# First expert layer computed batch by batch, with its returns gathered by token and the second block's first queries made beneath it

## The chip, the cores and the metric

The kernel runs on one core of one Trainium2 chip. The time is the device time of one execution in microseconds. The kernel before took 311.76 us (median of three runs: 332.05, 311.76, 310.14). Engines are called by the profile's names: PE is the matrix engine, DVE the vector engine, ACT the activation engine, POOL the general engine that here also issues the indexed DMAs, SP the engine that issues plain DMAs.

## The reference

Input x is 2 batches of 512 tokens of 128 values; the context is 2 batches of 77 tokens. Four layers follow each other, each added to x:

```
x = x + xattn0(layernorm(x), ctx)   # 16 heads of 8, rotary, distance bias, gated output
x = x + moe0(layernorm(x))          # 8 experts, 2 of them per token, no capacity limit
x = x + xattn1(layernorm(x), ctx)   # 16 heads of 8, plain
x = x + moe1(layernorm(x))          # 8 experts, 2 per token, capacity 321 rows per expert
```

An expert is `silu(x @ w1) @ w2` with w1 128x512 and w2 512x128. The first expert layer has biases and softmax weights over the two chosen logits:

```
gates = x @ Wg + bg
weights, indices = top_k(gates, 2); weights = softmax(weights)
h = silu(einsum('bsd,edf->bsef', x, W1) + b1)
all_out = einsum('bsef,efd->bsed', h, W2) + b2
out = sum(take_along_axis(all_out, indices) * weights)
```

There is no limit on how many tokens an expert gets, so the kernel holds a slower path for more than its buffers hold. On these inputs the reference's own routing of the first expert layer sends at most 173 tokens of batch 0 and 194 of batch 1 to one expert.

## The kernel before

Tokens lie in 8 tiles of 128, taken in 4 groups of 2 tiles (`GROUPS`); groups 0 and 1 are batch 0, groups 2 and 3 batch 1. Attention runs over 16 units (`UNITS`), 4 units of 4 heads for each group. In each unit PE makes scores, DVE takes their maxima (line 814, the row `peak`), PE makes shifted scores, ACT takes the exponential (line 669) and PE multiplies by the values (line 1224). The engines' instruction streams are written out separately and meet at semaphores. Tables (`PE_STEPS`, `DVE_STEPS`, `ACT_STEPS`, `POOL_STEPS`) say how many turns after a group's last unit a step of that group is put in each engine's stream: dividing by the sum and projecting (`attended`, `project`), the residual, the normalised input of the expert layer (`hidden`), its transpose (`turn`), the gate logits, `choose` (the two experts), `ranks` (a token's place in its expert's list), `slots`, and `send`. Every engine executes its stream strictly in order, so a step that waits holds everything written behind it.

An expert layer then goes so. POOL's `send` (line 527) scatters the rows, tile by tile, into a table `sent` in device memory with 384 rows per expert, each row carrying its pair number. When all 16 sends have landed, SP loads each expert's 384 rows. PE transposes them (line 1418), DVE splits them in a high and a low part (lines 988, 990), PE makes 12 matmuls of 384 columns (line 1431) and, after ACT's silu (line 706), the second product of 3 chunks by 4 (line 1442; each float32 matmul shows as two records). DVE adds the bias and POOL scatters the results by pair number into a table `back` (line 573). When all 24 scatters have landed SP loads `back` (`xe<-back`), and DVE combines (lines 1030, 1034), normalises, and the second block's queries are made: tokens transposed, projected, split (`low`), and stacked (line 1344). Then the second attention begins. All of it is strictly one after the other for the whole of both batches, except that the second block's keys are made before the experts. `overflows` reads the fullest expert's count behind the experts and branches over the slow path if it is at most 384.

The second block's w1 and w2 are loaded once the first experts are through; ACT copies a high part of w1 (line 642) and POOL makes the low part (line 542) inside the second attention.

## Time and profile before

| what | us |
|---|---|
| profiled execution, device time | 307.54 |
| its span in the trace | 305.8 |
| median of the three runs | 311.76 |
| PE busy | 231.1 (76% of the span) |
| DVE busy | 158.0 (52%) |
| ACT busy | 115.9 (38%) |
| POOL busy | 143.2 (47%) |

Busy shares are means over stages. The page's slices show PE almost full in both attentions and both expert layers, and nearly idle between an attention and its experts and between the first experts and the second attention. The chain of waits is the view that says what such a gap waits for. Times inside the kernel are microseconds from the span's start.

### The profile page before, as it was taken

The numbers are of one execution on the slowest core, as the hardware profiler recorded it, in microseconds if no ns is written. First come the engines' busy times: TensorE is split into PE (matmuls) and PEld (weight loads), VectorE is DVE, ScalarE is ACT, GpSimd is POOL, SyncE is SP. The second block draws the span as 40 slices with busy tenths as digits, with TensorE's granted clock in tenths as the row PEclk, the third lists the DMA queues.
The fourth block names the chain that finished last, engine by engine and source line by source line (L and its number), as shares of the span: only waits on it lengthen the run. The fifth ranks groups of instructions, "written<-read, shape, count | busy, mean of one in ns | idle before, by whom it ended". The sixth has DMA issues, their size and how long they took to land.

```text
span 305.8 us, 5311 instructions
## 1 busy us (share of the span) xinstructions
PE 231.1 (76%) x1952; PEld 187.6 (61%) x1952; DVE 158.0 (52%) x503; ACT 115.9 (38%) x202; POOL 143.2 (47%) x203
## 2 busy tenths in 40 slices
PE   2776799998935468999953878899987169999900
PEld 1655676766623358999952665556555059999900
DVE  2887446486585464434212864477986222343206
ACT  4024547765401025252500167975721104424200
POOL 5634800881533731565661500681567711655640
PEclk9999999999975559999995899999999758999985
DMA  7999990200000135000015920100011161001115
GB/s 227 298 196 380 273 205 11 72 3 0 28 17 27 45 95 139 23 28 16 31 44 150 390 85 2 53 18 2 17 37 35 36 166 53 27 28 34 32 44 174
DMA packets 26962, 27.07 MB, mean 89 GB/s; under 512 B 3208, under 2 KB 23987, under 8 KB 26677
## 3 DMA queue, kind: packets, MB, share of 16 engines
q1 hardware_dynamic: 23941, 21.64, 26.0%
q0 software_dynamic: 2560, 4.08, 4.1%
q10 hardware_dynamic: 432, 0.98, 1.0%
q8 instruction: 17, 0.28, 0.4%
q14 instruction: 12, 0.10, 0.1%
HBM read 16.82 MB, written 10.79 MB: 90 GB/s over the span
## 4 chain that ended last, share of the span: by engine, by line
PE 51%; DVE 18%; DMA 9%; issue 8%; POOL 7%; ACT 5%; POOLq 1%; SPq 0%; DVEq 0%; ACTq 0%
PE ps L1442 14%; PE ps L1431 11%; PE ps L1224 6%; PE ps L1201 5%; DVE stats L793 2%; PE ps L1156 2%; DMA xres<-x 2%; PE ps L1207 2%; POOL sent L527 2%; DMA xe<-back 2%; PE ps L1176 2%; PE ps L1418 2%; DMA sent<-hidk,slotu 2%; DVE norm L1030 1%; PE ps L1247 1%
## 5 line engine op out<-in xcount | busy, mean ns | idle before, releaser
L573 POOL DMA_INDIRECT back<-probT,pairu x48 | 46.5, 969 | 34.6 <-DVE probT L1001 15.1
L1442 PE MATMUL ps<-w,hT 128*128 128x128 f32 (+1 forms) x384 | 45.0, 274 | 0.0
L1442 PEld LDWEIGHTS ps<-w,hT 128*128 128x128 f32 (+1 forms) x384 | 44.2, 183 | 0.0
L1156 PE MATMUL ps<-blank,identr 128*128 128x256 f32 x90 | 27.7, 466 | 19.1 <-DMA sent<-hidk,slotu 10.3
L669 ACT ACTIVATE probT<-ps 77x1024 f32<-77x1024 f32 x32 | 32.6, 1020 | 24.8 <-PE ps L1207 16.8
L527 POOL DMA_INDIRECT sent<-hidk,slotu x32 | 32.0, 1000 | 17.5 <-issue 9.2
L542 POOL TENSOR_TENSOR w1lo<-hT,w1hi 128x256 fp32r<-128x256 f32 x32 | 23.8, 751 | 34.7 <-ACT w1hi L642 32.7
L814 DVE TENSOR_REDUCE peak<-ps 128x8 fp32r<-128x616 f32 x32 | 25.4, 794 | 23.3 <-PE ps L1176 23.1
L1156 PEld LDWEIGHTS ps<-blank,identr 128*128 128x128 f32 x90 | 20.5, 237 | 23.6 <-issue 11.3
L1201 PE MATMUL ps<-qst,kst 100*78 100x256 f32 x128 | 29.2, 301 | 4.2 <-ACT qst L652 3.4
L706 ACT ACTIVATE hT<-ps 128x321 f32<-128x321 f32 x32 | 14.1, 441 | 33.5 <-PE ps L1431 33.3
L706 ACT ACTIVATE hT<-ps,col 128x384 f32<-128x384 f32 x32 | 17.2, 582 | 22.7 <-PE ps L1431 22.7
L1201 PEld LDWEIGHTS ps<-qst,kst 100*78 100x78 f32 x128 | 16.8, 148 | 13.5 <-ACT qst L652 12.8
L1431 PE MATMUL ps<-xhi,w1hi 128*128 128x384 f32 (+1 forms) x64 | 22.8, 357 | 1.5 <-DVE xlo L990 1.5
L1431 PE MATMUL ps<-xhi,w1lo 128*128 128x384 f32 (+1 forms) x64 | 21.5, 335 | 0.0
L1431 PE MATMUL ps<-xlo,w1hi 128*128 128x384 f32 (+1 forms) x64 | 21.5, 335 | 0.0
L1224 PE MATMUL ps<-probT,vpad 77*32 77x256 f32 x256 | 20.4, 391 | 0.5 <-ACT cst L664 0.5
L509 POOL TENSOR_SCALAR vare<-mv 128x2 f32<-128x2 f32 (+2 forms) x17 | 3.8, 226 | 35.2 <-DVE mv L796 35.2
L1224 PE MATMUL ps<-probT,onepad 77*32 77x256 f32 x256 | 19.7, 379 | 0.0
L1001 DVE TENSOR_TENSOR probT<-ps,row 128x128 f32<-128x128 f32 x24 | 7.0, 291 | 24.1 <-PE ps L1442 24.1
L1004 DVE COPY probT<-ps 128x128 f32<-128x128 f32 (+1 forms) x24 | 7.0, 290 | 22.8 <-PE ps L1442 22.8
L1207 PE MATMUL ps<-btok,bkey 98*78 98x128 f32 x128 | 17.3, 229 | 0.0
(166 smaller groups left out, 450.6 us busy)
## 6 DMA issues: line engine op xcount, KB each, us to landing
sent<-blank SPq DMA_DIRECT2D x16, 193.5 KB, 8.4
xe<-sent SPq DMA_DIRECT2D x16, 193.5 KB, 4.1
back<-blank SPq DMA_DIRECT2D x16, 128.0 KB, 5.6
hT<-w1b SPq DMA_DIRECT2D x4, 512.0 KB, 6.0
w<-w2b SPq DMA_DIRECT2D x1, 2048.0 KB, 13.1
xe<-back SPq DMA_DIRECT2D x8, 256.0 KB, 3.6
hT<-w1d SPq DMA_DIRECT2D x4, 512.0 KB, 4.3
w<-w2d SPq DMA_DIRECT2D x1, 2048.0 KB, 10.3
```

Of the source, the lines that this page charges most:

```text
L527: pool.indirect_dma_start(sent[m], bass.IndirectOffsetOnAxis(ap=slotu[:, t, k:k + 1], axis=0), hidk[:, t, k, :], None, bounds_check=NSLOT ...
L542: part = pool.tensor_tensor(w, raw[:, k % RAWS, e, half], w1hi[:, PIECE * k + e, half].bitcast(F32), ALU.subtract)
L573: pool.indirect_dma_start(back[m], bass.IndirectOffsetOnAxis(ap=pairu[0:n, e, c:c + 1], axis=0), ye[0:n, e, c, :], None, bounds_check=NPAI ...
L669: act.activation(probT[0:KV, u % RING].rearrange("p (i q) t -> p i (q t)", i=2), ps[0:KV, BK:BK + 2, :], ACT.Exp).then_inc(s_exp[a], 1)
L706: act.activation(hT[:, e % 2, f, 0:CAP[m]], ps[:, 2 + n % 4, 0:CAP[m]], ACT.Silu, bias=bias).then_inc(s_silu[m], 1)
L814: dve.tensor_reduce(peak[:, u % 2], s, AX.X, ALU.max, negate=True).then_inc(s_peak[a], 1)
L1156: pe.matmul(ps[:, bank, 0:GQ], ident, blank[:, 0:2, 0:D], start=True, stop=True)
L1201: last = pe.matmul(ps[0:KP, BK + q // 2, GQ * (q % 2):GQ * (q % 2) + GQ], kst[0:ST + Q4, b, Q4 * j + q, :], qst[0:ST + Q4, j, at:at + GQ], ...
L1207: last = pe.matmul(ps[0:KP, BK + q // 2, o:o + P], bkey[0:LOW + NEAR, t, :], btok[0:LOW + NEAR, t, :], start=False, stop=(i == GT - 1))
L1224: last = pe.matmul(ps[32 * q:32 * q + 32, BND, den * GQ:den * GQ + GQ], w, probT[0:KV, u % RING, q, :], start=(j == 0 and not den), stop=( ...
L1431: last = pe.matmul(ps[:, 2 + n % 4, 0:EVEN[m]], w[:, e, f * P:(f + 1) * P], x[:, e % 2, 0:EVEN[m]], start=(i == 0), stop=(i == len(parts) ...
L1442: last = pe.matmul(ps[0:n, 6 + k % 2, c * P:(c + 1) * P], hT[:, e % 2, f, c * P:c * P + n], w2[:, e, f, :], start=(f == 0), stop=(f == FC ...
```

## The change

- The first expert layer works batch by batch, with tables `sent_b` of 8 x 208 rows for each batch (`CAP_B`, two chunks of 104 rows). An expert of one batch is cut in two halves (`half`); 18 halves make a batch. The list `TAIL` puts batch 0's halves between the last steps of groups 2 and 3 and the second block's keys. Batch 0's rows are sent earlier (`POOL_STEPS`, send 10 and 9 turns behind, and the steps ahead of it earlier to match).
- The list `SECOND` puts the sums, norms, tokens, queries and stacks of groups 0 and 1 of the second block between batch 1's halves. Those of groups 2 and 3 come inside the second attention (turns 5 to 11), where units 8 and 9 are no longer scored ahead.
- Results are written by slot into `made_b` with plain DMAs by SP, and POOL gathers each token's two rows (`fetch`, 16 indexed DMAs) into SBUF. The pair numbers, the 24 scatters and the 4 loads of `back` of the first layer are gone. A token without a slot gets the zero row behind the table.
- The count of the fullest expert of a batch is read in the middle of `TAIL`; the branch over the slow path stands between the two batches and compares with 208.
- The copy of the rows by ACT and the warm-up matmuls around the first experts are gone. The softmax weight comes from POOL as a power of e. The weight splits move to other turns (`HIGH_TURNS`, `LOW_TURNS`).
- The second expert layer is as before.

PE at the end of the first attention (`ps` is the accumulator, `xe` the experts' rows, `hT` the hidden values). Before, all steps of all groups come first, then warm-ups, and the experts:

```order
L1301 MATMUL ps<-khi,identr 32x156 x2
L1301 MATMUL ps<-klo,identr 32x156
L1156 MATMUL ps<-blank,identr 128x256 x3
L1418 MATMUL ps<-identr,xe 128x128 x6
L1431 MATMUL ps<-xhi,w1hi 128x384
L1431 MATMUL ps<-xlo,w1hi 128x384
L1431 MATMUL ps<-xhi,w1lo 128x384
L1431 MATMUL ps<-xhi,w1hi 128x384
```

Now the last group's projection is followed at once by batch 0's rows, and ranks of group 2 come between its halves:

```order
L1371 MATMUL ps<-qhi,qlo 128x256
L1372 MATMUL ps<-sqw,attT 128x256
L1502 MATMUL ps<-identr,xe 128x104 x4
L1510 MATMUL ps<-xhi,w1hi 128x208
L1510 MATMUL ps<-xlo,w1hi 128x208
L1510 MATMUL ps<-xhi,w1lo 128x208
...
L1401 MATMUL ps<-picked,tri 128x8
L1401 MATMUL ps<-picked,ones 128x8
L1401 MATMUL ps<-picked,tri 128x8
L1502 MATMUL ps<-identr,xe 128x104 x2
```

Batch 0's experts moved ahead of the routing of groups 2 and 3. The overflow branch of PE, behind the experts before, now has batch 1's rows behind it.

DVE in the second attention. Before, the first units stand among stackings, and no combining is left:

```order
L814 TENSOR_REDUCE peak<-ps 128x8
L974 SCALAR_TENSOR_TENSOR qlo<-ps,col,qhi 128x256
L814 TENSOR_REDUCE peak<-ps 128x8
L980 CAST qst<-ps 96x2x256
L814 TENSOR_REDUCE peak<-ps 128x8
L980 CAST qst<-ps 96x2x256
L814 TENSOR_REDUCE peak<-ps 128x8 x6
L823 RECIPROCAL cst<-cst 128x256
L824 TENSOR_TENSOR attT<-cst 128x256
```

Now the combination of group 2 (`norm<-xe,wtok,xres`, `xres<-xe,wtok,norm`) stands behind the sixth unit's maxima, and its norm and `qlo` behind the next two:

```order
L916 TENSOR_REDUCE peak<-ps 128x8 x6
L1152 SCALAR_TENSOR_TENSOR norm<-xe,wtok,xres 128x128 x2
L1156 SCALAR_TENSOR_TENSOR xres<-xe,wtok,norm 128x128 x2
L895 BN_STATS stats<-xres 128x6 x2
L898 BN_AGGR mv<-stats 128x2 x2
L916 TENSOR_REDUCE peak<-ps 128x8
L908 TENSOR_SCALAR norm<-xres,mv,rstd 128x128 x2
L916 TENSOR_REDUCE peak<-ps 128x8
L1073 SCALAR_TENSOR_TENSOR qlo<-ps,col,qhi 128x256
L1079 CAST qst<-ps 96x2x256
```

Combining, normalising and splitting moved in among the maxima; group 3's copy of the same follows at turn 8.

POOL behind the sends of the first layer (`L567`, `L573`: pair numbers and scatters). Before:

```order
L527 DMA sent<-hidk,slotu 3072x129 x4
L509 TENSOR_SCALAR vare<-mv 128x2
L510 TENSOR_TENSOR rstd<-vare,power 128x2
L527 DMA sent<-hidk,slotu 3072x129 x8
L567 CAST pairu<-xe 128x3 x8
L573 DMA back<-probT,pairu 2048x128 x24
L509 TENSOR_SCALAR vare<-mv 128x2
L510 TENSOR_TENSOR rstd<-vare,power 128x2
```

Now:

```order
L582 DMA sent_batch<-hidk,slotu 1664x128 x8
L604 TENSOR_TENSOR wexp<-euler,wdif 128x8
L597 DMA xe<-made_batch,slotu 128x128 x8
L560 TENSOR_SCALAR vare<-mv 128x2
L561 TENSOR_TENSOR rstd<-vare,power 128x2
L560 TENSOR_SCALAR vare<-mv 128x2
L561 TENSOR_TENSOR rstd<-vare,power 128x2
L597 DMA xe<-made_batch,slotu 128x128 x8
L560 TENSOR_SCALAR vare<-mv 128x2
L561 TENSOR_TENSOR rstd<-vare,power 128x2
```

The gathers of batch 0 (8) and batch 1 (8) took the place of 24 scatters, and the two variances of each batch stand behind that batch's gathers.

The diff, cut to its core:

```diff
+SB = 2
+PB = 104
+CAP_B = SB * PB
+NSLOT_B = E * CAP_B
+GB = GROUPS // B
...
-PE_STEPS = [dict(project=4, turn=8, logits=9, ranks=10, next_context=8, next_parts=10, next_keys=11,
-                 turn3=6, logits3=8, ranks3=9),
-            dict(project=4, turn=7, logits=7, ranks=9)]
-DVE_STEPS = [dict(attended=5, projected3=6, residual3=6, hidden3=8, projected=7, residual=7, hidden=9,
-                  choose=11, slots=12, next_context=12, next_parts=13, next_keys=14, choose3=10, slots3=11),
-             dict(attended=5, residual=7, hidden=8, choose=10, slots=11)]
-ACT_STEPS = [dict(tanh3=4, tanh=5, copies=8, turned=8),
-             dict(copies=9, turned=7)]
-POOL_STEPS = [dict(deviation=9, residual=12, send=14),
-              dict(deviation=5, residual=7, send=10)]
+PE_STEPS = [dict(ranks=(9, 7.5, 0, 0), project=(3.5, 3.5, 4.5, 0), turn=(6, 6, 0, 0), logits=(6.5, 6.5, 0, 0)),
+            dict(project=(6, 4, 4, 4), turn=(9, 7, 7, 7), logits=(9, 7, 7, 7), ranks=(10, 9, 9, 9))]
+DVE_STEPS = [dict(choose=(9, 8, 0, 0), slots=(10, 8, 0, 0), attended=(4, 4, 4, 0), projected=(6, 6, 6, 0),
+                  residual=(6, 6, 6, 0), hidden=(7, 7, 0, 0)),
+             dict(attended=(5, 5, 5, 5), residual=(9, 7, 7, 7), hidden=(10, 8, 8, 8), choose=(11, 10, 10, 10),
+                  slots=(12, 11, 11, 11))]
+ACT_STEPS = [dict(tanh=(4, 4, 5, 0), turned=(6, 6, 0, 0)),
+             dict(copies=(11, 9, 9, 9), turned=(9, 7, 7, 7))]
+POOL_STEPS = [dict(deviation=(6, 6, 0, 0), send=(10, 9, 0, 0)),
+              dict(deviation=(7, 5, 5, 5), residual=(9, 7, 7, 7), send=(12, 10, 10, 10))]
...
+              [(8.5, "tokens", 2), (9, "queries", 2), (9.5, "stack", 2),
+               (10.5, "tokens", 3), (11, "queries", 3), (11.5, "stack", 3)]]
...
+               [(5, "sum", 2), (6, "norm", 2), (7, "low", 2), (7, "stack", 2),
+                (8, "sum", 3), (9, "norm", 3), (10, "low", 3), (10, "stack", 3)]]
...
+TAIL = [("numden", 3), ("hidden", 2), ("attended", 3), ("turn", 2), ("turned", 2), ("logits", 2), ("project", 3), ("tanh", 3),
+        ("choose", 2), ("half", 0), ("half", 1), ("ranks", 2), ("projected", 3), ("residual", 3), ("slots", 2), ("half", 2),
+        ("half", 3), ("hidden", 3), ("turn", 3), ("turned", 3), ("half", 4), ("logits", 3), ("choose", 3), ("half", 5),
+        ("ranks", 3), ("slots", 3), ("half", 6), ("half", 7), ("next_context", 0), ("half", 8), ("most", 0), ("half", 9),
+        ("next_parts", 0), ("half", 10), ("half", 11), ("next_keys", 0), ("half", 12), ("half", 13), ("half", 14),
+        ("own_keys", 0), ("half", 15), ("half", 16), ("own_keys", 1), ("half", 17)]
...
+SECOND = [("half", 0), ("half", 1), ("half", 2), ("half", 3), ("half", 4), ("sum", 0), ("half", 5), ("half", 6), ("half", 7),
+          ("norm", 0), ("tokens", 0), ("half", 8), ("sum", 1), ("queries", 0), ("high", 0), ("half", 9), ("low", 0),
+          ("half", 10), ("stack", 0), ("half", 11), ("norm", 1), ("tokens", 1), ("half", 12), ("queries", 1),
+          ("high", 1), ("half", 13), ("low", 1), ("half", 14), ("stack", 1), ("half", 15), ("half", 16), ("half", 17)]
...
+LOW_TURNS = [[4, 5, 6, 10], [9, 11, 13, 17]]
...
+        sent_b = [nc.dram_tensor(f"sent_batch{b}", (NSLOT_B, D), F32, kind="Internal").ap() for b in range(B)]
+        made_b = [nc.dram_tensor(f"made_batch{b}", (NSLOT_B + 1, D), F32, kind="Internal").ap() for b in range(B)]
...
+            def rows_to_experts(b, e):
+
+                if b >= 1:
+                    sp.wait_ge(s_xT[0], E * (b - 1) + e + 1)
+                sp.dma_start(rows_b[:, e, :, :], sent_b[b][e * CAP_B:(e + 1) * CAP_B, :]
+                             .rearrange("(c p) d -> p c d", p=PB)).then_inc(s_xe[e], 16)
+
+            def rows_made(b, e):
+
+                sp.wait_ge(s_ye[0], SB * (E * b + e + 1))
+                sp.dma_start(made_b[b][e * CAP_B:(e + 1) * CAP_B, :].rearrange("(c p) d -> p c d", p=PB),
+                             ye_b[:, b, e, :, :]).then_inc(s_made[b], 16)
+
...
+            sp.wait_ge(s_sent_b[0], 16 * TB * K2)
+            for e in range(E):
+                rows_to_experts(0, e)
+            for e in range(PIECES):
+                rows_made(0, e)
+            sp.wait_ge(s_sent_b[1], 16 * TB * K2)
+            for e in range(PIECES):
+                rows_to_experts(1, e)
+            for e in range(PIECES, E):
+                rows_made(0, e)
+                rows_to_experts(1, e)
+            for e in range(E):
+                rows_made(1, e)
+            sp.wait_ge(s_down[0], SB * E * B)
+            for k in range(RAWS):
+                first_weights(1, k)
+            sp.dma_start(w2[:], w2d.rearrange("p (e c d) -> p e c d", e=E, c=FC)).then_inc(s_w2[1], 16)
+            for k in range(RAWS, PIECES):
+                first_weights(1, k)
+            sp.wait_ge(s_sum[0], TILES)
+            sp.wait_ge(s_sent, 16 * NPAIR // P)
...
+            def fetch(g):
+
+                b = g // GB
+                pool.wait_ge(s_made[b], 16 * E)
+                if g == 0:
+                    pool.wait_ge(s_blank_b, 16 * (E + 1) * B)
+                for i in range(GT):
+                    for k in range(K2):
+                        t = GT * g + i
+                        pool.indirect_dma_start(got_b[b][:, t % TB, k, :], None, made_b[b],
+                                                bass.IndirectOffsetOnAxis(ap=slotu[:, t, k:k + 1], axis=0),
+                                                bounds_check=NSLOT_B, oob_is_err=False).then_inc(s_fetched[g], 16)
+
+            def weights():
+
+                pool.wait_ge(s_dif[0], GROUPS)
+                pool.tensor_tensor(wexp[:], euler[:], wdif[:], ALU.pow).then_inc(s_wexp[0], 1)
 
             def residual(g):
...
+            send(0, 2)
+            send(0, 3)
+            weights()
+            for b in range(B):
+                for g in range(GB * b, GB * b + GB):
+                    fetch(g)
+                for g in range(GB * b, GB * b + GB):
+                    deviations(of_group(g))
             route(1)
...
+                    if a == 1 and u == RING // B:
+                        act.wait_ge(s_made[1], 16 * E)
...
+                    dve.scalar_tensor_tensor(out=slotu[:, s, :], in0=slot[:, s, :], scalar=float(NSLOT_B), in1=over[:, s, :],
+                                             op0=ALU.min, op1=ALU.max).then_inc(s_slot[m], 1)
...
+            def half(b, h):
+
+                e, second = divmod(h, 2)
+                if h == 0:
+                    split_rows(0, E * b, ps[:, ROWS, 0:CAP_B], CAP_B)
+                if not second:
+                    if e >= 2:
+                        batch_outputs(b, e - 2)
+                    if e + 1 < E:
+                        split_rows(0, E * b + e + 1, ps[:, ROWS, 0:CAP_B], CAP_B)
+                elif e == E:
+                    batch_outputs(b, E - 1)
...
+            def raised(m, x, e, f, bank, columns):
+
+                parts = ((w1hi, xhi), (w1hi, xlo), (w1lo, xhi))
+                for i, (w, rows) in enumerate(parts):
+                    last = pe.matmul(ps[:, bank, 0:columns], w[:, e, f * P:(f + 1) * P], rows[:, x % 2, 0:columns],
+                                     start=(i == 0), stop=(i == len(parts) - 1))
+                last.then_inc(s_up[m], 1)
+
+            def lowered(m, x, e, first, n, out):
+
+                for f in range(FC):
+                    last = pe.matmul(out, hT[:, x % 2, f, first:first + n], w2[:, e, f, :], start=(f == 0), stop=(f == FC - 1))
+                last.then_inc(s_down[m], 1)
+
+            def half(b, h):
+
+                e, second = divmod(h, 2)
+                x = E * b + e
+                if h == 0:
+                    if b == 0:
+                        pe.wait_ge(s_w2[0], 16)
+                        pe.wait_ge(s_w1lo[0], PIECES)
+                        pe.wait_ge(s_exp[0], UNITS)
+                        pe.wait_ge(s_nd[0], GROUPS)
+                    rows_in(x)
+                if not second and e + 1 < E:
+                    rows_in(x + 1)
+                for f in (2 * second, 2 * second + 1) if e < E else ():
+                    n = FC * x + f
+                    pe.wait_ge(s_xTsb[0], x + 1)
+                    if n >= UPS:
+                        pe.wait_ge(s_silu[0], n - UPS + 1)
+                    raised(0, x, e, f, UP + n % UPS, CAP_B)
+                if second and e >= 1:
+                    pe.wait_ge(s_silu[0], FC * x)
+                    for c in range(SB):
+                        k = SB * (x - 1) + c
+                        if k >= 2:
+                            pe.wait_ge(s_ye[0], k - 1)
+                        lowered(0, x - 1, e - 1, c * PB, PB, ps[0:PB, DOWN + k % 2, 0:D])
+
+            def keys(a, n):
+                stack_k(0)
+
+            fullest_of = []
+            steps = dict(most=lambda a, n: fullest_of.append(fullest(pe)), project=project, turn=turn, logits=logits, ranks=ranks, next_context=next_context,
+                         next_parts=next_parts, next_keys=next_keys, half=half, tokens=tokens_in, queries=project_q,
+                         stack=stack_q, keys=keys)
 
...
+                    query_steps(a, u + 2.5)
+                    if u + 1 == second and a == 1:
+                        scores(a, second)
+                        attend(a, second - AHEAD)
+                        maxima(a, second)
+                        scores(a, second + 1)
...
+            with pe.If(fullest_of[0] > CAP_B):
```

## Rows read from the trace of the kernel before

**Rows 1.** Windows; after the span of each: engine busy us, granted clock, DMA share, GB/s.
```profile
core 0: us, PE busy (x) PEld busy (x) DVE busy (x) ACT busy (x) POOL busy (x), PEclk, DMA share, GB/s
84.00:86.00 2.00, 1.35 (x20) 0.68 (x19) 1.80 (x9) 0.58 (x1) 0.16 (x1) 1.00 0.10 33
...
88.00:92.00 4.00, 1.40 (x4) 1.23 (x5) 3.04 (x7) 0.00 (x0) 2.17 (x3) 0.50 0.05 17
...
108.00:111.50 3.50, 2.07 (x24) 1.31 (x18) 1.08 (x6) 1.36 (x3) 1.45 (x2) 0.50 0.12 38
```

**Rows 2.** Timeline of PE, end of first attention to experts: start, us, engine, line, work [idle].
```profile
84.73 0.61 PE L1224 MATMUL ps<-probT,onepad 77*32 77x256 f32 x8
...
116.53 0.44 PE L1431 MATMUL ps<-xhi,w1hi 128*128 128x384 f32 x1 [0.95 <-DVE xlo L990]
```

**Rows 3.** Chain of waits in order of time: start, us, what ran.
```profile
124.35 2.12 PE ps L1431 x12
...
129.47 2.12 PE ps L1431 x12
...
151.73 5.37 PE ps L1442 x48
...
160.17 2.18 DMA back<-probT,pairu
162.37 3.47 DMA xe<-back
...
176.99 1.19 PE ps L1344 x8
...
264.86 1.82 PE ps L1431 x12
```

**Rows 4.** Timeline of PE inside the first attention.
```profile
44.50 0.29 PE L1207 MATMUL ps<-btok,bkey 98*78 98x128 f32 x2
44.63 0.29 PE L1201 MATMUL ps<-qst,kst 100*78 100x256 f32 x1
```

**Rows 5.** Timeline of DVE, end of the first block.
```profile
76.06 0.79 DVE L814 TENSOR_REDUCE peak<-ps 128x8 fp32r<-128x616 f32 x1
...
100.89 0.17 DVE L868 SCALAR_TENSOR_TENSOR logit<-ps,gbias 128x16 f32<-128x16 f32 x1 [2.33 <-PE ps L1265]
...
104.02 0.16 DVE L898 TENSOR_TENSOR slotu<-slot,over 128x4 uint32<-128x4 f32 x1
```

**Rows 6.** Timeline of POOL, sends of the last two groups.
```profile
99.36 1.07 POOL L527 DMA_INDIRECT sent<-hidk,slotu  x1 [2.47 <-DVE slotu L898]
...
108.79 0.97 POOL L527 DMA_INDIRECT sent<-hidk,slotu  x1 [0.30 <-issue]
```

**Rows 7.** Timeline of DVE, combining the first block.
```profile
157.12 0.29 DVE L1001 TENSOR_TENSOR probT<-ps,row 128x128 f32<-128x128 f32 x1 [0.60 <-PE ps L1442]
165.86 0.61 DVE L1030 SCALAR_TENSOR_TENSOR norm<-xe,wtok,xres 128x128 f32<-128x128 f32 x2 [8.44 <-DMA xe<-back]
...
167.84 0.58 DVE L1030 SCALAR_TENSOR_TENSOR norm<-xe,wtok,xres 128x128 f32<-128x128 f32 x2
```

**Rows 8.** Timeline of DVE, second attention and tail.
```profile
180.47 0.79 DVE L814 TENSOR_REDUCE peak<-ps 128x8 fp32r<-128x616 f32 x1
...
197.86 0.80 DVE L814 TENSOR_REDUCE peak<-ps 128x8 fp32r<-128x616 f32 x1 [1.58 <-PE ps L1176]
...
217.08 0.79 DVE L814 TENSOR_REDUCE peak<-ps 128x8 fp32r<-128x616 f32 x1
...
238.95 0.56 DVE L898 TENSOR_TENSOR slotu<-slot,over 128x4 uint32<-128x4 f32 x1
```

**Rows 9.** Timeline of POOL, low weights of the second block.
```profile
193.01 12.79 POOL L542 TENSOR_TENSOR w1lo<-hT,w1hi 128x256 fp32r<-128x256 f32 x16 [17.10 <-ACT w1hi L642]
```

**Rows 10.** Page, DMA issues: line's work, count, KB each, us from issue to landing.
```profile
w<-w2d SPq DMA_DIRECT2D x1, 2048.0 KB, 10.3
...
back<-probT,pairu POOLq DMA_INDIRECT x48, 2.2
```

610 lines of the change are left out of this document (313 added, 297 removed).

## The prediction

> **What bounds the kernel now.** I read the page's slices first, then the chain of waits, then the timelines of the engines around the places that the chain names. No engine is the bound over the whole span; it changes by stage. In both attentions and both expert layers PE is nearly full. Between them it is starved. The first such gap runs from PE's last product of the first attention to the first matmul of an expert, 85.3 to 116.5 us [rows 2]. In it PE does little, and its granted clock falls from 1.00 to 0.50, which is 1.2 instead of 2.4 GHz [rows 1]. The chain shows why: the last two groups must be projected, routed and sent, and eight sends of POOL at 9.43 / 7 = 1.35 us each stand at the end [rows 6]. The second gap runs from DVE's last expert output at 157.4 to the first maxima of the second attention at 180.5 [rows 7, 8]. It holds the last scatter's landing and the reload (160.2 to 165.8, [rows 3]), then four combinations 2.0 us apart [rows 7], and the norms, queries and stacks. Together the gaps are some 54 us. The change fills both with expert work of the other batch, and pays for it in matmuls and in the second attention.
>
> **The price of an expert of one batch.** Before, an expert takes 129.47 - 124.35 = 5.12 us of PE [rows 3]. An up matmul of 384 columns costs 2.12 / 12 = 0.177 us and one of 322 columns 1.82 / 12 = 0.152 [rows 3]. The line through both gives 0.106 at 208 columns. That is an extension below 322 columns; the end above is the 322-column price itself. In the first attention a pair of 128-column matmuls of the same kind starts 0.13 us ahead of the next row, 0.065 each [rows 4], so small ones do get cheaper, though with only 78 stationary columns. I take 0.11, so 12 x 0.11 = 1.3 us. The second product is now 2 chunks x 4 = 8 matmuls, 16 records at 5.37 / 48 = 0.112, so 1.8 us. The transposes take the rest of the 5.12, 5.12 - 2.12 - 24 x 0.112 = 0.3, two thirds of it now. Sum 3.4 us (ends 3.3 and 3.9). Sixteen of them are 54 us against 41 before: the change adds 13 us of PE work in all.
>
> **When batch 0 starts.** Its last slots now stand behind the last unit's maxima, 76.06 + 0.79 = 76.85 [rows 5]. Choosing and placing a group takes 104.18 - 100.89 = 3.3 us including PE's ranks [rows 5], so 80.2. Four sends put the last send's start at 84.6. From a last send's start to the first up matmul it is 116.53 - 108.79 = 7.7 us [rows 2, 6]. So batch 0 begins at 92, where before PE idled.
>
> **When the second attention starts.** Batch 0: 8 x 3.4 = 27.2. PE comes out of the gap at half clock [rows 1]; before, a warm-up bridged that, and now the first expert or so pays it: between 0 and 5 us, I take 2.5. The remaining tail work on PE (group 3's projection partly, two turns, logits, ranks, the keys), about 3.5 at full clock, is now between halves. That is 125. Meanwhile groups 2 and 3 are routed under the halves, their eight sends end near 107 to 110, and batch 1's rows lie ready long before 125. Between the batches the last outputs, the first rows' transposes and splitting cost 2, and the overflow branch 1: 128. Batch 1: 27.2, two stackings of 1.2 [rows 3], and 2 for transposes, projections and small waits: 160. The first maxima of the second attention then stand at 160 instead of 180.5: **20.5 us earlier**.
>
> What of it is hidden: the writes of `made_b` and batch 0's eight gathers (8 x 1.35 = 11 us of POOL from about 128) lie under batch 1's experts; if they came 10 us later, DVE would hold batch 1's outputs behind the first sum. The removed ACT copies and pair numbers cost nothing before, since ACT and POOL were idle there. The softmax weight by POOL is one small instruction behind the sends.
>
> **The branch.** No row shows it: PE, ACT and DVE took it in the idle 157.4 to 165.9 before the combine [rows 7]. So its price is between 0 and 8.4 us, and now all of it stands on PE's path. I take 1, because the count is read earlier and the rest is a jump. The Trainium skill, Runtime: NRT & Kernel Launch, section on instruction fetch mechanics, says that a taken branch to code outside the sequencer's window forces a DMA fetch before execution goes on. By that rule the term lies above my 1, somewhere toward the 8.4, and the time between this forecast and rival 2.
>
> **What the second attention pays.** Three terms. First, DVE gets the combinations of groups 2 and 3, 2 x 2.0 us [rows 7], and two norms. Before, these lay in the gap; here they stand among maxima, whose 16 units took 36.6 us [rows 8]. Some 5 us of work, of which I count 3, since a part fills DVE's waits (1.58 us before the maxima of the ninth unit, [rows 8]). Second, unit 8 can't be scored ahead: group 2 has to be transposed, projected, split and stacked first, a chain across PE, ACT and DVE of about two turns of (197.86 - 180.47) / 8 = 2.2 us [rows 8], of which one is normally covered; the same, smaller, at group 3. I take 3, ends 0 and 6. Third, the last quarter of the low weights, 12.79 / 4 = 3.2 us of POOL [rows 9], now stands at turn 17, ahead of group 1's sends; it delays the following variances by about 1. Sum **7 us** back.
>
> Group 2's rows must be there at DVE's turn 5, about 171. `made_b` of batch 1 lands at 163 (a plain transfer between device memory and SBUF took 3.5, [rows 3]), four gathers take 5.4, landing 2.2 [rows 10]: 171, just in time. But at 160 SP also issues the new w1 and w2, and w2 alone took 10.3 us to land [rows 10]. A gather that had to wait for all of that would come at up to 178. No run shows both at once, so 0 to 7 us; I take 0 within the 7 above. The Trainium skill, DMA: Bandwidth & Descriptors, section on queues, rings and completion order, says that each engine takes turns between queues packet by packet. By that rule a gather is slowed but not queued behind the load, and the sum stays as it is.
>
> From the first maxima on, everything else is as before: 305.8 - 180.5 = 125 us. **Sum:** 307.5 - 20.5 + 7 = 294 us. That is against the profiled execution (307.54, span 305.8), which is 1.4% below the shown median of 311.76; I predict from the profiled one. What can be told from no change is 2%, so faster means below 305.5 and slower above 318.
>
> **Rivals.**
> 1. *More gain, 284 us.* The split of work inside the second attention costs nothing (DVE idle before several maxima, [rows 8]), and the clock is back at once. Then 7 and 2.5 drop out. Against it: DVE executes in order, and PE waits for `norm` of group 3 behind both a combination and a reciprocal. Chance 0.15.
> 2. *Branch and bulk load, 302 us.* The upper ends: 8.4 for the branch instead of 1, or 7 for gathers behind the weights. Either adds 7 to 8. For it: neither is visible anywhere; against: each end is a whole gap. Chance 0.10. The Trainium skill's rule on taken branches (Runtime: NRT & Kernel Launch, above) speaks for the first of the two.
> 3. *The overlap is not had, 305 us.* DVE's first half of batch 0 stands ahead of group 3's `projected`, and PE's ahead of ranks of group 2. If batch 0's rows come late, as with the sends of group 1 where they were (10 us later), routing and experts wait for each other in turn: plus 9 for the start and 2 for the holes. The change then doesn't do what it says. Against it: all steps of group 1 were moved up. Chance 0.10.
> 4. *Slower, 320 us.* The gather. Only scatters are in the trace, at 1.35 us. If a gather held POOL for c, the last rows of group 3 would be there at 128 + 16c + 2 and are needed at 178. It stands alone at the end from c = 3, and loses the 24 us to 318 from c = 4.5; 320 is c = 4.6. A gather that held POOL until it landed would take 1.0 + 2.2 = 3.2 and still cost only 3. Chance 0.08.
>
> That the slow path runs is excluded: at most 194 rows of a batch go to one expert, below 208.
>
> **How the numbers follow.** The forecast, 294 with its own range 287 to 300, has 0.57. The range 280 to 306 takes in rivals 1 and 2, and the lower part of 3, and leaves out 4, the rest of 3 and little at the lower end. Faster: 0.57 + 0.15 + 0.10 and half of rival 3, less some for the unknown, 0.80. Same: 0.12. Slower: 0.08.
>
> **What would show it.** First up matmul of batch 0 near 92; 3.4 us per expert; no wait for rows at batch 1; the first maxima of the second attention near 160, and the sixteenth 42 to 43 us behind it. PE's clock at 1.00 within some microseconds of the start of batch 0. PE idle for 2 to 4 us between the batches. Wrong if an up matmul of 208 columns costs 0.15 or more (plus 8 us), if POOL spaces its gathers over 3 us apart, or if the second attention takes 50 us.

## The result: slower by 8%, where faster by 5% was forecast

| | before | after |
|---|---|---|
| median, us | 310.95 (309.17 to 332.05) | 334.49 (332.49 to 336.20) |
| ratio to before | | 1.0775, 95% interval 1.0682 to 1.0869 |
| span of the profiled execution, us | 305.8 | 332.7 |
| mean granted clock in it | 0.90 | 0.786 |

Some executions of each kernel run in a slower state; ratios leave them out, and a difference of two runs is given as a range where it changes without them. The spans differ by 26.9 us. Three landmarks of DVE divide them: the first and the sixteenth maxima of the second attention, and the end.

| | before | forecast | after |
|---|---|---|---|
| first up matmul of batch 0 | | 92 | 103.1 |
| last matmul of batch 0 | | 125 | 136.6 |
| first matmul of batch 1 | | 128 | 140.6 |
| first maxima of the second attention | 180.5 | 160 | 174.2 |
| its sixteen maxima take | 36.6 | 42.6 | 64.1 |
| from the last of them to the end | 88.7 | 89.7 | 94.4 |

Of the 7 us that the prediction gives to the second attention, 6 are work among its maxima; the seventh, POOL's low weights, stands behind them.

### The profile page after: what moved, and what is told of

It is laid out like the page before. It is cut to its first block, busy times and chain, and to the rows that moved or that the text cites. A ratio compares the mean times of both kernels' runs of the same rounds, so it can differ in the third digit from the quotient of the medians.

```text
span 332.7 us, 5693 instructions
## 1 busy us (share of the span) xinstructions
PE 272.1 (82%) x2074; PEld 213.6 (64%) x2074; DVE 166.9 (50%) x528; ACT 122.4 (37%) x229; POOL 134.9 (41%) x189
## 4 chain that ended last, share of the span: by engine, by line
PE 67%; DVE 14%; issue 5%; DMA 5%; POOL 5%; ACT 3%; SPq 0%; POOLq 0%; DVEq 0%
PE ps L1517 14%; PE ps L1510 12%; PE ps L1346 11%; PE ps L1322 7%; PE ps L1297 3%; PE ps L1466 3%; PE ps L1328 2%; DMA xres<-x 2%; POOL sent L585 2%; PE ps L1282 2%; PE ps L1390 2%; DVE cst L925 2%; PE ps L1372 2%; PE ps L1502 1%; PE ps L1307 1%
## 5 line engine op out<-in xcount | busy, mean ns | idle before, releaser
L1517 PE MATMUL ps<-w,hT 128*104 128x128 f32 (+2 forms) x448 | 52.7, 273 | 0.5 <-ACT hT L791 0.5
L1517 PEld LDWEIGHTS ps<-w,hT 128*104 128x104 f32 (+2 forms) x448 | 50.3, 172 | 0.6 <-ACT hT L791 0.6
L754 ACT ACTIVATE probT<-ps 77x1024 f32<-77x1024 f32 x32 | 32.6, 1020 | 44.1 <-PE ps L1322 25.2
L791 ACT ACTIVATE hT<-ps,col 128x208 f32<-128x208 f32 x64 | 25.1, 433 | 31.8 <-PE ps L1510 30.9
L1510 PE MATMUL ps<-xhi,w1hi 128*128 128x208 f32 (+1 forms) x96 | 32.2, 335 | 0.6 <-DVE xlo L1095 0.6
L597 POOL DMA_INDIRECT xe<-made_batch,slotu x16 | 16.3, 1016 | 37.3 <-DMA made_batch<-probT 33.0
L1510 PE MATMUL ps<-xlo,w1hi 128*128 128x208 f32 (+1 forms) x96 | 29.2, 305 | 0.0
L646 POOL DMA_INDIRECT back<-probT,pairu x24 | 23.2, 966 | 14.8 <-DVE probT L1128 11.8
L1510 PE MATMUL ps<-xhi,w1lo 128*128 128x208 f32 (+1 forms) x96 | 29.2, 304 | 0.0
L617 POOL TENSOR_TENSOR w1lo<-hT,w1hi 128x256 fp32r<-128x256 f32 x32 | 23.5, 736 | 13.0 <-ACT w1hi L722 11.1
L1297 PE MATMUL ps<-kst,qst 96*128 96x312 f32 x64 | 20.9, 417 | 0.8 <-ACT qst L833 0.8
L1510 PEld LDWEIGHTS ps<-xhi,w1hi 128*128 128x128 f32 x96 | 20.2, 210 | 1.7 <-DVE xlo L1095 0.9
## 6 DMA issues: line engine op xcount, KB each, us to landing
w<-w2b SPq DMA_DIRECT2D x1, 2048.0 KB, 10.8
w<-w2d SPq DMA_DIRECT2D x1, 2048.0 KB, 11.8
```

The source lines that it names most:

```text
L597: pool.indirect_dma_start(got_b[b][:, t % TB, k, :], None, made_b[b], bass.IndirectOffsetOnAxis(ap=slotu[:, t, k:k + 1], axis=0), bounds_c ...
L617: part = pool.tensor_tensor(w, raw[:, k % RAWS, e, half], w1hi[:, PIECE * k + e, half].bitcast(F32), ALU.subtract)
L646: pool.indirect_dma_start(back, bass.IndirectOffsetOnAxis(ap=pairu[0:n, e, c:c + 1], axis=0), ye[0:n, e, c, :], None, bounds_check=NPAIR - ...
L754: act.activation(probT[0:KV, u % RING].rearrange("p (i q) t -> p i (q t)", i=2), ps[0:KV, BK:BK + 2, :], ACT.Exp).then_inc(s_exp[a], 1)
L791: act.activation(hT[:, x % 2, f, 0:CAP_B], ps[:, UP + (FC * x + f) % UPS, 0:CAP_B], ACT.Silu, bias=col[:, V_B1 + FC * e + f:V_B1 + FC * e ...
L1297: last = pe.matmul(ps[:, BS + i, 0:Q4 * KP], qst[0:ST, j, at + i * P:at + (i + 1) * P], kst[0:ST, b, Q4 * j:Q4 * j + Q4, :].rearrange("p q ...
```

## The profile after

From the page, the busy tenths of PE and its granted clock in 40 slices of 8.3 us:

```profile
PE   2867899988888999499997999789999708999910
...
PEclk9998999995555999879996555575556967999975
```

Before, the clock was at 0.5 in and just behind the gaps ahead of the first experts, the second attention and the second experts, and nearly full in between. Now it is at 0.50 (1.2 GHz) in slices 10 to 13, and at 0.5 to 0.7 in the ten from 22 to 31, which are the whole second attention and its last steps. PE is shown as busy for 7 to 9 tenths there: busy, and slow. Windows show how it gets there (columns as in [rows 1]):

```profile
core 0: us, PE busy (x) PEld busy (x) DVE busy (x) ACT busy (x) POOL busy (x), PEclk, DMA share, GB/s
73.00:76.00 3.00, 0.36 (x6) 0.22 (x4) 2.74 (x9) 1.02 (x1) 0.57 (x2) 0.75 0.00 0
76.00:80.00 4.00, 4.00 (x27) 2.41 (x28) 1.41 (x3) 0.84 (x3) 3.19 (x4) 0.50 0.10 33
...
172.00:176.00 4.00, 2.90 (x25) 2.43 (x24) 1.83 (x5) 0.90 (x3) 0.00 (x0) 1.00 0.39 74
176.00:180.00 4.00, 3.37 (x16) 2.33 (x16) 1.43 (x2) 2.11 (x3) 2.50 (x3) 0.61 0.89 297
...
184.00:188.00 4.00, 4.00 (x32) 2.10 (x24) 1.19 (x3) 1.38 (x2) 2.51 (x3) 0.50 0.78 287
```

Twice the same thing happens. PE has a sparse stretch (0.36 us of 3 at 73, 2.90 and 3.37 of 4 from 172), the clock goes from 1.00 to 0.50, and then it stays there for long though PE is shown busy 4.00 of 4 in many windows: until 108 the first time, until 216 the second. The timeline of PE gives the causes:

```profile
76.00 0.38 PE L1307 MATMUL ps<-identr,peak 128*4 128x128 f32 x2 [2.64 <-DVE peak L916]
...
103.10 0.52 PE L1510 MATMUL ps<-xhi,w1hi 128*128 128x208 f32 x1
...
132.91 3.66 PE L1517 MATMUL ps<-w,hT 128*104 128x128 f32 x32
140.64 0.58 PE L1502 MATMUL ps<-identr,xe 104*128 104x104 f32 x2 [4.08 <-issue]
...
175.18 0.28 PE L1307 MATMUL ps<-identr,peak 128*4 128x128 f32 x2 [0.98 <-DVE peak L916]
```

At 73 PE waits 2.64 us for the maxima of the fifteenth unit (unit 14, counted from 0), because DVE has written in front of them the slots of group 0, for which it first waits 3.01 us for PE's ranks, and the residual and variances of group 1, steps that the change moved up. At 136.6 there are 4.08 us in which the profile shows nothing that PE waits for: the boundary of the batches, with the branch. At 174 the second attention starts with units that hold nothing but scores and maxima. Before, the first four units had two stackings and a projection of batch 1's queries between them; these now come at turns 8.5 to 11.5.

The timeline of DVE, for [rows 8], and of POOL, for [rows 6]:

```profile
174.24 0.80 DVE L916 TENSOR_REDUCE peak<-ps 128x8 fp32r<-128x616 f32 x1
...
187.61 0.61 DVE L1152 SCALAR_TENSOR_TENSOR norm<-xe,wtok,xres 128x128 f32<-128x128 f32 x2 [0.29 <-DMA xe<-made_batch,slotu]
...
206.90 0.80 DVE L916 TENSOR_REDUCE peak<-ps 128x8 fp32r<-128x616 f32 x1 [1.00 <-PE ps L1297]
...
238.33 0.79 DVE L916 TENSOR_REDUCE peak<-ps 128x8 fp32r<-128x616 f32 x1
...
267.55 0.56 DVE L1006 TENSOR_TENSOR slotu<-slot,over 128x4 uint32<-128x4 f32 x1
```

```profile
176.89 1.13 POOL L597 DMA_INDIRECT xe<-made_batch,slotu  x1 [16.47 <-DMA made_batch<-probT]
178.32 1.00 POOL L597 DMA_INDIRECT xe<-made_batch,slotu  x1 [0.31 <-issue]
...
272.74 0.97 POOL L585 DMA_INDIRECT sent<-hidk,slotu  x1 [0.30 <-issue]
```

The ninth maxima (206.90) come 12.84 us behind the eighth (194.06); before, that distance was like the others, 2.4. A gather occupies POOL for 1.00 us and the next follows 1.30 behind: the gather is no burden to POOL. The lines of the second attention (174 to 238) show the slow matmuls: the 100x78 scores take 430 ns each (296 before, 180 to 217), the 77x32 products 627 (391 before).

```profile
L1322 PE MATMUL ps<-qst,kst 100*78 100x256 f32 x56 | 15.7, 430 | 1.3 <-ACT qst L732 1.2
...
L1346 PE MATMUL ps<-probT,vpad 77*32 77x256 f32 x88 | 11.7, 627 | 0.0
```

## The experiments

Theory 1: the clock is what was lost, at the start of the stage, since the 12 idle matmuls ahead of it are gone. Theory 2: the work moved into the stage cost the time. Theory 3: the clock, but lost by the stage's own gaps. Theory 4: something beside it, such as the bulk load, takes the clock. Theory 5: the chain of batch 1's queries is too long for the place it has. "Ratio" is to the kernel before, run on the same chip, with its 95% interval. "Sixteen maxima" is from the first to the last in the profiled execution. `warm_up(n, bank)` issues n idle matmuls, each of which shows as two records.

### The clock

**e1_warm_second**
```diff
             for name, n in SECOND: ...
+            warm_up(12, 3)
             attention(1)
```


> The changed kernel with the 12 idle matmuls put back between the experts of batch 1 and the second attention (the kernel before had them there, the change took them out). Theory 1 (the clock is what was lost in the second attention; its granted clock is 0.50 from 179 to 254 because TensorE came into it with too little work): the stage is entered at 1.00 and stays there, the 16 peak reductions take some 45 us in place of 64, and the run is 12 to 20 us shorter than the changed kernel's 334.5: 315 to 323. Theory 2 (the sums, norms and queries moved into the stage and the gap at unit 8 cost the time): nothing but 3 us of idle matmuls is added, about 337. Theory 3 (the clock is lost within the stage, by its own gaps, not at its start): clock 1.00 at first, then 0.50 again from the gap at unit 8 on: 325 to 332.

Measured: 347.86 us (342.31 to 348.69; no interval). The idle matmuls ran for 5.35 us at full clock, the stage began at 180.6, and from 187 the clock was at 0.50 as before. Sixteen maxima: 64.6 us. Theory 1 falls; dense work just ahead of the stage does not carry over. All three numbers of the expectation were missed.

**e2_before_cold**
```diff
-WARM_SUM = 12
+WARM_SUM = 0
```


> The kernel before without its 12 idle matmuls ahead of the second attention. Theory 1: the queries of the second attention are then made at 0.50 and the attention, whose units leave TensorE few gaps but are sparse, stays at 0.50 for much of its 60 us: 320 to 335, about what the changed kernel takes. Theory 2: the queries alone run slow, 2 to 3 us, less what the idle matmuls took: 309 to 313.

Measured: 321.88 us, but from 307.49 to 332.12, so nothing can be said of the time (the kernel before itself goes from 306 to 326 beside it). The profile, of an execution of 315.68 us, is clearer:

```profile
184.00:188.00 4.00, 3.90 (x15) 3.18 (x16) 1.93 (x5) 1.19 (x3) 0.40 (x1) 0.50 0.51 217
188.00:192.00 4.00, 3.24 (x20) 2.60 (x20) 2.10 (x4) 2.90 (x7) 0.00 (x0) 0.87 0.01 2
192.00:196.00 4.00, 3.12 (x24) 2.35 (x23) 2.58 (x4) 2.96 (x7) 0.00 (x0) 1.00 0.00 0
```

The queries were made at 0.50. They brought the clock back by the first maxima (190.55), and the old stage kept it at 1.00 to its end. Sixteen maxima: 36.6 us, exactly as with the idle matmuls. So the old order held the clock without them. Theory 1 falls a second time.

**e4_hole**
```diff
+                    if a == 0 and u + 1 == 14:
+                        warm_up(10, BMX)
                     if u + 1 < UNITS ...: maxima(a, u + 1)
```


> The changed kernel with the 10 idle matmuls at unit 14 of the first attention alone. Theory 1: 6 to 12 us under the changed kernel (323 to 329), with the second attention at 0.50 as before; e1's and e4's gains add up to e3's. Theory 2: 334 to 336.

Measured: 330.64 us, ratio 1.0749 (1.0591 to 1.0908): 3.9 us under the changed kernel, short of the 6 to 12, and the intervals overlap.

```profile
80.00:84.00 4.00, 4.00 (x63) 2.74 (x61) 2.07 (x17) 2.40 (x3) 0.97 (x1) 1.00 0.11 34
84.00:88.00 4.00, 1.72 (x14) 1.12 (x14) 2.31 (x4) 0.15 (x1) 2.56 (x3) 0.97 0.10 33
88.00:92.00 4.00, 3.39 (x32) 1.30 (x24) 2.37 (x9) 2.29 (x4) 2.42 (x4) 0.50 0.11 35
```

The hole is closed and the clock full until PE's next wait, 2.29 us for `attT`. The first up matmul comes at 98.55 and the first maxima at 170.3, 4.6 and 3.9 us earlier. That is the hole's price by the traces; the ratios do not resolve it. The stage was at 0.50 from 176 to 212, and then the clock came back for its last units: sixteen maxima 60.1 us.

**e3_warm_second_hole** (both edits)

> e1, and 10 idle matmuls into the bank of the maxima ahead of the maxima of unit 14 of the first attention, where TensorE waited 2.64 us for VectorE and its clock fell to 0.50 for the next 32 us. Theory 1: the first block's end and batch 0's first experts come at 1.00; 2.6 + 32/2 in the bound case, against waits on VectorE that stay: 6 to 12 us under e1. Theory 2: within 1 us of e1.

Measured: 336.24 us, ratio 1.0913 (1.0694 to 1.1131): 10 to 12 us under e1, in the expected 6 to 12. Its sixteen maxima ended at 238.1, the clock coming and going within them.

**e5_early**
```diff
+                    if a == 1 and u <= 4: warm_up(3)
                     if u < UNITS: shifted_scores(a, u)
+                    if a == 1 and u <= 4: warm_up(1, BMX)
```
and four ahead of the first maxima.

> The changed kernel with idle matmuls in the waits of the first five units of the second attention alone: 4 ahead of the first maxima, and in each of units 0 to 4 three ahead of the shifted scores and one behind them. e1 showed that work just ahead of the stage does not hold its clock: it fell 5 us into the stage, where TensorE waits 0.7 to 1.0 us in each unit. Theory 3 (the clock is lost by the stage's own gaps, since the queries that filled these units now stand under the experts): clock 1.00 up to the gap at unit 8, a unit in 2.3 to 2.7 us in place of 3.78, 8 to 14 us under the changed kernel: 320 to 327. Theory 4 (something else, such as the bulk load of weights at 444 GB/s beside it, takes the clock): 0.50 from 177 to 180 on as before, 334 to 338.

Measured: 334.08 us (328.40 to 337.31; no interval). Windows of its second attention:

```profile
176.00:180.00 4.00, 4.00 (x26) 3.43 (x25) 1.14 (x2) 1.57 (x3) 2.30 (x3) 1.00 0.95 303
180.00:184.00 4.00, 4.00 (x26) 3.49 (x25) 1.25 (x2) 1.55 (x3) 3.08 (x4) 1.00 1.05 427
184.00:188.00 4.00, 4.00 (x36) 2.85 (x34) 0.80 (x1) 1.44 (x3) 2.73 (x3) 1.00 0.77 298
```

The clock holds at 1.00 beside a load of 427 GB/s. So the gaps of the units lose it, and theory 4 falls. It held until the gap at unit 8 (0.50 from 208 on), as theory 3 said. But the time did not come back, and the 320 to 327 was missed: the units with four idle matmuls took 2.66 us and those with the sum and norm beside them 3.9. Where PE was no longer slow, it was waiting or idling on purpose.

**e6_early_bubble** (and idle matmuls at unit 8: 3 ahead of its scores, 4 ahead of its maxima, 2 in each of four units behind)

> e5 and idle matmuls at unit 8 (3 ahead of its scores, 4 ahead of its maxima, 2 in each of the four units behind it). Theory 3: the stage stays at 1.00 to its end, its 16 peaks take 44 to 48 us: 308 to 318. Theory 4: no gain over e5, 0 to 3 us more.

Measured: 329.11 us, ratio 1.0622 (1.0479 to 1.0765). The clock was 1.00 from 148 to 236, and the sixteen maxima still took 58.5 us, not 44 to 48, and the run not 308 to 318.

**e7_all_holes** (and the 10 of e4, and 10 ahead of `project(0, 2)`)

> e6, the 10 idle matmuls at unit 14 of the first attention (e4), and 10 more ahead of the projection of group 2 of the first block, where TensorE waited 2.3 us for VectorE and e4's clock fell to 0.50 until 106. Theory 3: the clock is 0.50 only at the boundary of the batches; 4 to 10 us under e6: 300 to 312, at best level with the kernel before. Theory 4: 330.

Measured: 327.54 us, ratio 1.0582 (1.0443 to 1.0721); sixteen maxima 58.4 us. The 300 to 312 was missed. The run with most of its clock restored (mean 0.897, as before) is still 6% slower. What the maxima then wait for is in its chain of waits (start, us, what ran):

```profile
195.97 0.09 ACT w1hi L722
...
196.93 0.58 ACT cst L740
197.50 0.92 ACT probT L754
...
199.79 0.37 ACT inT L818
...
201.00 0.48 ACT qhi L828
...
201.51 0.49 DVE qlo L1073
...
202.05 1.18 PE ps L1468 x8
...
204.84 0.80 DVE peak L916
```

The tokens of group 2 wait behind other copies on ACT, then go ACT, PE, ACT, DVE, PE, DVE, one behind the other, and unit 8's maxima at the end, 9.8 us behind unit 7's. Group 3 does it again (6.9 us).

**e8_heavy** (five idle matmuls in units 0 to 6, 4 and 6 at unit 8, 4 behind)

> e7 with more: five idle matmuls in each of units 0 to 6, 4 and 6 at unit 8, 4 in each of the four behind it. Tells whether e6's clock is lost for too little of them: if e6 and e7 hold 1.00, this is 2 to 5 us slower than e7; if they don't, it is faster than e7.

Measured: 335.80 us, ratio 1.0869 (1.0725 to 1.1014): 6 to 8 us slower than e7, more than the expected 2 to 5. e7's filling was enough; more is only load.

### The chain of the queries

**e9_light_fill** (6 at unit 14; 4 ahead of the first maxima; 2 ahead of the shifted scores of units 0 to 5; 2 and 2 at unit 8. The 2 in each of the four units behind it, named in the expectation, are not in the kernel: the edit has `pass` there.)

> The changed kernel with lighter filling: 6 idle matmuls at unit 14 of the first attention, 4 ahead of the second attention's first maxima, 2 ahead of the shifted scores of units 0 to 5, 2 and 2 at unit 8, 2 in each of the four units behind it. It stands as the pair of e10. Theory 3 (clock): 320 to 328. Theory 5 (at a full clock the second attention is still 20 us longer than before, since the queries of batch 1 are now made in it as one chain over PE, ACT and DVE at units 8 and 11): its 16 peaks take 52 to 58 us even where the granted clock is 1.00.

Measured: 323.65 us, ratio 1.0407 (1.0321 to 1.0492), within the 320 to 328: the best of all variants of the changed kernel. With half of e7's filling in the second attention it came out 4 to 7 us under e7; the two intervals just touch. The clock was full up to unit 8 and 0.50 from 204 on; sixteen maxima 59.7 us, over the 52 to 58 (profiled execution 326.30 us).

**e10_light_fill_early_chain**
```diff
-[(8.5, "tokens", 2), (9, "queries", 2), (9.5, "stack", 2), (10.5, "tokens", 3), ...
+[(7.5, "tokens", 2), (8, "queries", 2), (8.5, "stack", 2), (9.5, "tokens", 3), ...
-HIGH_TURNS = [..., [5, 6, 9, 15]]
+HIGH_TURNS = [..., [4, 5, 11, 15]]
```
and likewise on ACT and DVE.

> e9 with the chain of batch 1's queries put one to one and a half units earlier on PE, ACT and DVE (sum of group 2 at turn 4 in place of 5, its tokens at 7.5 in place of 8.5, group 3's sum at 7 in place of 8, its tokens at 9.5 in place of 10.5), and the 1.05 us conversions of second weights on ACT moved away from it (turns 4, 5, 11, 15 in place of 5, 6, 9, 15). Theory 5: the gap ahead of unit 8's peak (9.8 us in e7 from the peak of unit 7) falls to 5 to 7, and that at unit 11 (6.9 us) to 3 to 5: 5 to 9 us under e9. Theory 3 alone: no difference over 2 us.

Measured: 330.57 us, ratio 1.0714 (1.0642 to 1.0787), 7 to 10 us slower than e9 instead of 5 to 9 faster. The two profiled executions differ by only 1.8 us, so they do not hold the whole difference. A row of DVE and one of PE show what went wrong:

```profile
184.10 0.61 DVE L1152 SCALAR_TENSOR_TENSOR norm<-xe,wtok,xres 128x128 f32<-128x128 f32 x2 [4.93 <-DMA xe<-made_batch,slotu]
...
204.37 0.69 PE L1282 MATMUL ps<-identr,norm 128*128 128x128 f32 x2 [3.96 <-DVE norm L908]
```

At turn 4 group 2's gathered rows are not back. DVE waits 4.93 us in order, and the maxima behind it with it. So the chain can't start at turn 4: the gathers begin only when batch 1's last rows are written (176.89 in the changed kernel). The edit also put group 3's tokens (turn 9.5) ahead of unit 8's scores on PE, which waited 3.96 us for their norm. The gap ahead of the ninth maxima grew to 14.0 us from e9's 9.1, where 5 to 7 was expected. So the run does not test an earlier chain alone.

**e11_early_chain** (the same, without idle matmuls)

> The earlier chain of e10 in the changed kernel, without idle matmuls. Theory 5: 3 to 7 us under the changed kernel (a ratio of 1.055 to 1.07 to the kernel before, the changed kernel's being 1.0775), the stage still at 0.50 for most of it. If the chain only matters once the clock is full, a ratio of 1.07 to 1.08.

Measured: 327.96 us, ratio 1.0625 (1.0543 to 1.0706). Inside the expected 1.055 to 1.07, but its interval touches the changed kernel's. Its sixteen maxima took 58.6 us with the clock back at 1.00 from 204 to 208 and from 216 to 232; that, rather than the earlier chain, may be the gain. Not settled.

**e15_conversions_away**
```diff
-HIGH_TURNS = [..., [5, 6, 9, 15]]
+HIGH_TURNS = [..., [3, 4, 12, 15]]
```
with the 6 idle matmuls at unit 14.

> The changed kernel with the 6 idle matmuls at unit 14 of the first attention, and ACT's 1.05 us conversions of second weights at turns 3, 4, 12, 15 in place of 5, 6, 9, 15: those two that stood ahead of the queries' chain (inT and qhi of group 2) are gone from it. The chain's share alone: 1 to 3 us under e4's ratio (1.075), so 1.065 to 1.075.

Measured: 331.89 us, ratio 1.0804 (1.0670 to 1.0938). The ninth maxima came 12.85 us behind the eighth (191.52 to 204.37), as in the changed kernel, and the ratio is above the expected 1.065 to 1.075. ACT's conversions were not what delayed it.

**e13_queries_ahead**
```diff
 SECOND = [..., ("half", 17),
+          ("warm", 0), ("sum", 2), ("norm", 2), ("tokens", 2), ("queries", 2), ("sum", 3), ("high", 2),
+          ("low", 2), ("norm", 3), ("stack", 2), ("tokens", 3), ("queries", 3), ("high", 3), ("low", 3), ("stack", 3)]
-PE_QUERIES[1], ACT_QUERIES[1], DVE_QUERIES[1] = ...
+PE_QUERIES[1], ACT_QUERIES[1], DVE_QUERIES[1] = [], [], []
```


> The changed kernel with one part undone: the sums, norms and queries of batch 1 (groups 2 and 3) are made ahead of the second attention, as in the kernel before, not at its turns 5 to 11.5; TensorE waits for group 2's gathered rows and then runs the 12 idle matmuls, as the kernel before did. First maxima come when batch 1's rows are back (187) and the queries made: 194 to 197 in place of 174. Theory 5 (the chain in the stage costs some 20 us even at a full clock) with theory 3 (its sparse units lose the clock): the 16 peaks then take 36 to 40 us in place of 64, granted clock 1.00 throughout, the last peak at 231 to 236 in place of 238.3, and the run 2 to 7 us shorter than the changed kernel (ratio 1.055 to 1.07): the overlap that the change bought with the stage's order gave nothing. If the stage was long for another reason (the gathers or the bulk load beside it), the peaks take 50 us or more and the run is 5 to 15 us longer.

Measured: 362.07 us, ratio 1.1773 (1.1642 to 1.1905). Windows, and the first and last maxima:

```profile
196.00:200.00 4.00, 2.21 (x13) 1.34 (x11) 1.14 (x4) 0.99 (x3) 0.00 (x0) 1.00 0.00 0
200.00:204.00 4.00, 1.88 (x4) 0.79 (x4) 0.91 (x2) 1.28 (x3) 0.00 (x0) 0.56 0.00 0
204.00:208.00 4.00, 2.77 (x13) 2.42 (x13) 1.51 (x3) 1.75 (x2) 0.00 (x0) 0.50 0.00 0
```

```profile
206.84 0.78 DVE L916 TENSOR_REDUCE peak<-ps 128x8 fp32r<-128x616 f32 x1
...
262.94 0.78 DVE L916 TENSOR_REDUCE peak<-ps 128x8 fp32r<-128x616 f32 x1
```

Two expectations failed. The queries were ready at 206.8, not 197: idle matmuls begun at half clock took 8.37 us, and the chain in the open some 11 more. So making them inside the stage does gain: it starts 32.6 us earlier and pays 8. And the clock did not hold: the sixteen maxima took 56.1 us at 0.50 with no chain and no idle matmuls in them, against 36.6 at 1.00 before. That is not the clock's price alone, since e13 keeps the changed order at unit 8:

```profile
227.35 0.80 DVE L916 TENSOR_REDUCE peak<-ps 128x8 fp32r<-128x616 f32 x1 [2.97 <-PE ps L1297]
236.12 0.80 DVE L916 TENSOR_REDUCE peak<-ps 128x8 fp32r<-128x616 f32 x1 [7.97 <-PE ps L1297]
```

The queries of unit 8 are ready, and its maxima, the ninth, still come 8.77 us behind unit 7's (2.38 before). Since unit 8 is not scored ahead, PE first multiplies the values of two earlier units and makes the shifted scores of unit 7, and DVE waits.

**e14_queries_ahead_hole** (e13 and the 6 idle matmuls at unit 14)

> e13 and the 6 idle matmuls at unit 14 of the first attention. Theory 3: another 3 to 5 us less, a ratio of 1.04 to 1.055.

Measured: 357.59 us, ratio 1.1612 (1.1521 to 1.1702). The 4.5 us under e13 are the expected 3 to 5; the ratio missed with e13's.

**e16_queries_ahead_filled** (e13 with 2 to 6 idle matmuls at each step of the chain, four ahead of the first maxima, two ahead of the shifted scores of units 1 to 9, two or one behind those of units 0 to 9)

> e13 with idle matmuls in the waits of the queries' chain (2 to 6 at a time) and of units 0 to 9 (two ahead of the shifted scores, one or two behind). e13's clock fell to 0.50 while it made those queries and stayed there, and its 16 peaks took 56.1 us with no chain in the stage. Theory 3: here the clock holds at 1.00 and the 16 peaks take 38 to 44 us; the difference of 12 to 18 us is the clock's alone, and the run is 10 to 18 us under e13's 362: 344 to 352. If the peaks still take over 50 us at 1.00, the clock is not what e13's stage lost.

Measured: 354.44 us, ratio 1.1474 (1.1367 to 1.1581).

```profile
212.00:220.00 8.00, 8.00 (x61) 6.31 (x59) 2.83 (x4) 4.14 (x6) 0.00 (x0) 1.00 0.01 3
...
228.00:236.00 8.00, 8.00 (x79) 5.30 (x78) 0.80 (x1) 6.35 (x8) 2.92 (x4) 1.00 0.11 24
```

The clock stayed at 1.00 until 256, and the sixteen maxima took 48.1 us (209.45 to 257.56), 8.0 less than e13 but not 38 to 44, with 22.3 us of PE's busy time in idle matmuls. The distance to the ninth maxima was still 7.54 us. The run was 7.6 us under e13, short of the 10 to 18. What the stage would take at full clock without idle matmuls no run shows.

### The branch, and the kernel before

**e12_no_overflow**
```diff
-            with pe.If(fullest_of[0] > CAP_B):      # and the same on ACT and DVE
+            if False:
```


> The changed kernel with the overflow part left out on all engines (the branch on the fullest expert and all behind it; with these inputs nothing of it is run). It prices the boundary of the batches, where TensorE ends batch 0's last matmul at 136.5 and begins batch 1's first at 140.64 with 3.73 us that the profile shows no wait for. If that is the branch: the gap falls to 0.5 us, the clock doesn't fall there (0.50 from 138 to 145 in the changed kernel), and the run is 5 to 8 us shorter: a ratio of 1.05 to 1.065. If it is the way of the rows (DVE's last outputs, then the transposes), the gap stays and the ratio is 1.07 to 1.08.

Measured: 330.64 us, ratio 1.0727 (1.0653 to 1.0801). PE's first matmul of batch 1:

```profile
136.16 0.40 PE L1502 MATMUL ps<-identr,xe 104*128 104x104 f32 x2 [0.40 <-DVE probT L1103]
```

The idle time ahead of it falls from 4.08 to 0.40 us. The branch costs 3.7 us of PE, and the first maxima come at 169.4, 4.8 earlier. The intervals of the two ratios overlap. The clock fell behind the boundary all the same (0.69 from 140 to 144), and the second attention was at 0.50 again, so only that much was gained, less than the 5 to 8.

**e17_before_fill_sends** (the kernel before; its second experts start at half clock too)
```diff
+                if m == 1:
+                    warm_up(34, 2)
                 pe.wait_ge(s_sent[m], 16 * NPAIR // P)
-                warm_up(WARM_ROWS[m], 2)
+                warm_up((3, 8)[m], 2)
```


> The kernel before with 34 idle matmuls ahead of its second wait for the sent rows (TensorE waited 8.65 us there and the second experts then ran at 0.50 until 255) and 8 in place of 3 behind it. Theory 3: the second experts begin at 1.00, 2 to 4 us under the kernel before, a ratio of 0.985 to 0.995. If the clock doesn't hold, or the experts wait for VectorE's splits anyway, no difference.

Measured: 321.01 us, ratio 1.0358 (1.0261 to 1.0454): slower. In its profile the clock fell in the second attention's tail, at 224, where the kernel before had 1.00, and why it fell there, ahead of the edit, is open. The 34 idle matmuls ran for 15.7 us, from 246.4 to 262.2, at 0.63 from 248 to 252 and then at 1.00; the first rows were back at 255.8 (POOL's first pair numbers), so they also held PE some 6 us too long.

No version beat the kernel before.

## Why the prediction was wrong

The span forecast was 294 less 1.7 around it, 292.3. The table at the top divides the 40.4 us to 332.7 (rounded): 11.1 at the start of batch 0, 0.5 within it, 1.1 at the boundary, 1.6 in batch 1, 21.5 in the sixteen maxima, 4.7 behind them.

**The step that failed is "What the second attention pays. Sum 7 us back"**, with the sentence behind it, that from there everything is as before. It counted work added to the stage and took its speed as given. From the first to the sixteenth maxima it measured 27.5 us more than before. By the distances between the maxima, 4.8 of these lie up to the eighth, 10.5 between the eighth and the ninth, 7.0 in the next four distances and 5.2 in the last three. The runs divide them so:

- The chain of queries and the sums: 64.1 - 56.1 = 8.0 us (the changed kernel against e13), or 60.1 - 55.5 = 4.6 with the hole at unit 14 filled (e4 against e14). Forecast were 6, so this work was priced well. Of the 8.0, 4.1 are at unit 8 and 4.5 at unit 11; the rest cancels.
- The order at unit 8: the distance of the ninth maxima stays at 8.77 us in e13 and 7.54 in e16, against 2.38, although neither has the chain. For order and chain at unit 8 together the forecast gave 3, at most 6; it measured 10.5. No run scores unit 8 ahead with the rest changed, so this share is read from the traces, not tested.
- The clock: e13, at 0.50, took 19.5 us more than the kernel before; that holds unit 8's order too, and 2.4 us in the last three distances, which stay at full clock (11.5 in e6, e7 and e16, against 9.1). Restoring the clock gave back 8.0 (e13 to e16), net of the idle matmuls' own cost. So here the clock is worth at least 8 us and at most 17. The forecast did not price it at all.

**The clock was counted at one place only**, 2.5 us for "the first expert or so". The prediction saw it fall in the old gaps and asked how fast the new start would recover. It did not ask which new holes the change makes. There were three: 2.64 us at unit 14 (price 4.6 us at batch 0's first up matmul, by e4), the boundary, and the emptied first units of the second attention. Of the removed idle matmuls it spoke at the first experts only; that they had guarded the second attention was theory 1, and e1 and e2 refute it. That the emptied units are what lost the clock rests on e5 and e16, which filled them; putting the old stackings back there was not tried.

**When batch 0 starts**: 103.1 instead of 92. 4.6 us came back with the hole filled (e4). Group 1's last maxima were only 1 us late, but from there to its slots it took 9.7 us, not 3.3: DVE waited 4.33 us for PE's gate logits and 2.99 for its ranks (2.00 and 1.13 in e4), which the forecast left out. The last send of group 1 began at 92.28 in the changed kernel and 88.81 in e4, not 84.6, and from there it was 10.8 and 9.7 us to the first up matmul, not 7.7: PE has the projections and the turn of the later groups ahead of the first half. Both are the order that the change itself wrote; the prediction assumed that PE would be free. Rival 3 gave 9 us for such a late start, but not its other half: routing and experts did not hold each other up.

**The price of an expert** was right: at full clock it took 3.44 us with its transposes (149.07 to 152.51), against 3.4. The terms as written add to 3.3 only; over 16 experts that is 1.6 us. Batch 0 took 33.5 us against 33, and batch 1 to the first maxima 33.6 against 32.

**The branch**: 3.7 us (e12) against 1, but the rest of the boundary took 0.4 against 2. The price lies between the forecast and rival 2's 8.4; by the trace the wait has no releaser, only "issue". The Trainium skill's rule (Runtime: NRT & Kernel Launch, instruction fetch mechanics), that a taken branch outside the sequencer's window forces a fetch, put it in that interval; no run here shows that the time is a fetch.

**The gathers**: 1.30 us apart, so rival 4 is refuted. Beside the bulk load of weights the first four took 6.8 to 7.0 us to land, against 2.6 for most of batch 0's, and DVE waited 0.29 us for them, so the 7 us of rival 2 are not there either. By the rule of the Trainium skill cited there (DMA: Bandwidth & Descriptors, on queues, rings and completion order) a gather is slowed but not queued behind the load; the trace agrees: the first landed at about 183.7, the load's second part, issued at 176.0, 11.8 us later at 187.8. That the slower landing cost so little is partly luck, since the stage itself was slow: at the old pace (10.5 us for five units) DVE would have come to the sum near 185.5 and waited some 2 us for rows that were there at 187.6. This is an estimate from these rows.

**Behind the last maxima**: 94.4 us instead of 89.7. From the last slots to the last send's start it was 5.2 us, exactly as before (267.55 to 272.74, and 238.95 to 244.14), and from there to the end 60.0 against 61.7. What grew is the way from the sixteenth maxima to the last slots, 29.2 us against 21.9; the clock was at 0.50 there until 252, where before it was at 1.00. POOL's 3.2 us of low weights at 252.28 held group 1's send for 2.6 us. No run parts the two.

**The chances**: 0.08 for slower, all of it on one mechanism that did not occur. The section on what would prove it wrong did name a second attention of 50 us; it gave that no weight.

## What to carry to other kernels

Before moving work out of a stage that is "full", look at what the stage's own units look like without it: the filling between dependent steps can be what keeps TensorE at 2.4 GHz, and a stage of small matmuls may not bring it back once it is lost. Price a reordering twice, once at each of the clock's levels for every stage that it touches, and list the new waits of PE as carefully as those that go. Where a unit can no longer be prepared ahead, count everything that now stands in front of it, not only what it newly depends on: here 10.5 us more stood between two maxima. Idle matmuls inside the waits did hold the clock here, but they cost much of what they saved; ahead of the stage they did nothing.

## What the runs showed of the hardware

- A stage can run at 0.50 for over 50 us with PE shown busy 3.35 to 4.00 of each 4 us (e13, 208 to 264). In the changed kernel 100x78 matmuls of 256 columns then take 430 ns in the profile on average instead of 296, and a unit 3.78 us instead of 2.2.
- The old stage came from 0.50 back to 1.00 within 8 us while PE was busy 3.90 and 3.24 of 4 (e2, 184 to 192); the new one lost it at 3.37 of 4 (176 to 180) and did not regain it at 4.00 of 4 (184 to 204). With the same order of the stage e4 had it back at 1.00 from 216 to 224, and the changed kernel only at 0.77 and 0.66 there. So the busy time in the profile does not tell which way it will go.
- A body that is not run still costs: 3.7 us of PE at a branch on a register whose value was read long before (e12).
- A gather of 128 rows took 2.6 us to land alone and up to 7.0 beside a load of some 440 GB/s; it held POOL for 1.00 us either way.
